# Graph attention on one core: the columns of the q and k weights reordered, and one transfer per block where there were four

## The reference, cut to what matters

```python
h = maximum(layernorm(x), 0)
q, k, v = split_heads(h @ Wq + bq), split_heads(h @ Wk + bk), split_heads(h @ Wv + bv)
scores = einsum('bhqd,bhkd->bhqk', q, k) / sqrt(32) + beta * adj
scores = where(adj > 0, scores, -9e15)
out = x + merge_heads(softmax(scores) @ v)
```

## Time and profile before

| what | value |
|---|---|
| median of 3 runs | 1079.25 us (1078.97 to 1079.58) |
| the profiled execution's own time | 1079.27 us |
| its span, first to last instruction | 1077.4 us |
| granted PE clock, mean | 0.992 of full |
| PE busy | 1020.8 us, 95% |
| DVE busy | 967.6 us, 90% |
| ACT busy | 884.5 us, 82% |
| POOL busy | 567.5 us, 53% |
| transfers of q and k into the stacks | 768 in the whole run |

### The profile page before, as it was taken

One profiled execution on the slowest core, in us unless ns is written; L12 is line 12 of the kernel. 1 busy time (PEld: TensorE's weight loads), 2 busy tenths in 40 slices (PEclk: granted clock), 3 DMA queues, 4 the chain that ended last, 5 costly groups with the idle time before them and its releaser, 6 DMA issues. The chain is left out here.

```text
span 1077.4 us, 33776 instructions
## 1 busy us (share of the span) xinstructions
PE 1020.8 (95%) x10959; PEld 709.7 (66%) x10959; DVE 967.6 (90%) x4343; ACT 884.5 (82%) x2343; POOL 567.5 (53%) x756
## 2 busy tenths in 40 slices
PE   3899999999999999999999999999999999999986
PEld 2466676666666666666666667666666666667664
DVE  6579998999899999999999999999999999999897
ACT  3378888888888888888888888888888888888887
POOL 3645655445665445565444565544565544565431
PEclk9899999999999999999999999999999999999997
DMA  5454445554444554444554444554444554444441
GB/s 156 108 132 129 113 127 139 158 134 127 107 133 132 157 138 129 111 129 136 150 140 132 111 130 129 150 145 134 130 107 132 144 150 134 130 104 135 117 116 41
DMA packets 91038, 138.79 MB, mean 129 GB/s; under 512 B 15600, under 2 KB 66288, under 8 KB 90864
## 3 DMA queue, kind: packets, MB, share of 16 engines
q1 hardware_dynamic: 90336, 135.85, 47.1%
q10 hardware_dynamic: 528, 0.79, 0.2%
HBM read 35.91 MB, written 25.17 MB: 57 GB/s over the span
## 5 line engine op out<-in xcount | busy, mean ns | idle before, releaser
L523 ACT ACTIVATE probs<-biased,neg_max 128x128 f32<-128x128 f32 x1536 | 490.5, 390 | 146.9 <-DVE neg_max L638 115.5
L437 PE MATMUL ps_p<-hT,w 128*128 128x512 f16 x1728 | 423.5, 382 | 23.9 <-DVE hT L609 18.7
L638 DVE CUSTOM_DVE_ANT_0 biased<-ps_s,mask 128x128 f32<-128x128 f32 x1536 | 353.5, 286 | 75.8 <-PE ps_s L458 74.5
L336 POOL TENSOR_TENSOR on<-on,xb 128x384 f32<-128x384 f32 x128 | 128.0, 1000 | 380.9 <-DVE on L659 380.1
L437 PEld LDWEIGHTS ps_p<-hT,w 128*128 128x128 f16 x1728 | 167.5, 98 | 175.7 <-DVE hT L609 26.1
L644 DVE TENSOR_TENSOR pT<-ps_t,pT 128x512 f16<-128x512 f32 x384 | 263.3, 686 | 0.9 <-ACT pT L548 0.9
L466 PE MATMUL ps_t<-ident,probs 128*128 128x128 f32 x1536 | 245.4, 283 | 0.1
L548 ACT ACTIVATE pT<-ps_t 128x512 f16<-128x512 f32 x384 | 220.5, 574 | 1.0 <-PE ps_t L466 1.0
L437 PE MATMUL ps_p<-w,hT 128*128 128x384 f16 x1152 | 207.6, 326 | 0.0
L458 PEld LDWEIGHTS ps_s<-k_st,q_st 96*128 96x128 f16 x1536 | 117.5, 97 | 81.3 <-DVE neg_max L638 6.9
L481 PE MATMUL ps_o<-v,pT 128*128 128x33 f16 x1536 | 157.1, 179 | 8.9 <-DVE pT L644 5.2
(11 more groups left out here) (62 smaller groups left out, 1016.8 us busy)
## 6 DMA issues: line engine op xcount, KB each, us to landing
q_st<-qT SPq DMA_DIRECT2D x384, 96.0 KB, 2.2
k_st<-kT SPq DMA_DIRECT2D x384, 96.0 KB, 2.2
out<-on SPq DMA_DIRECT2D x128, 192.0 KB, 2.1
xs<-in_x SPq DMA_DIRECT2D x31, 768.0 KB, 5.0
adjs<-in_adj SPq DMA_DIRECT2D x32, 256.0 KB, 5.0
xs<-in_x ACTq DMA_DIRECT2D x1, 768.0 KB, 7.1
k_st<-in_L_gnn_Wq SPq DMA_DIRECT2D x1, 576.0 KB, 5.6
k_st<-in_L_gnn_Wk SPq DMA_DIRECT2D x1, 576.0 KB, 9.3
```

The lines of the kernel that those rows point to most:

```text
L336: pool.tensor_tensor(on[:, j % 2, :], on[:, j % 2, :], xb[:, par, j, :], ALU.add).then_inc(added, 1)
L437: mm = pe.matmul(dst, stationary, moving, start=m == 0, stop=m == MMS - 1)
L523: act.activation(probs[:, odd, i, :], biased[:, odd, i, :], ACT.Exp, bias=neg_max[:, odd, i:i + 1], scale=-1.0).then_inc(exp_done, 1)
L638: dve.tensor_tensor_reduce(out=biased[:, odd, i, :], in0=ps_s[:, i * N:(i + 1) * N], in1=mask[:, gp, v // CH, :], scale=-1.0, scalar=3.0e3 ...
```

## The change

Columns of the q and k weights (and of their bias rows) are written in another order: old column 96i + e becomes new column 4e + i, for i from 0 to 3 and e from 0 to 95. So in column group c, partition 4d + i holds dimension d of head 3i + c. The four heads of a stack's block are then interleaved over all 128 partitions of `qT`, in the order in which 32 partitions by 4 heads are stored in `q_st`, and one transfer moves them. A step has 3 transfers for q and 3 for k. The chunk c of a graph now holds heads c, 3 + c, 6 + c, 9 + c in place of 4c to 4c + 3. The split of the weights is done in three pieces, one per row group, on ACT and on DVE, for v's too; for q's and k's the raw weights are read with a step of 96 elements between neighbours.

```diff
+        def heads_first(row):
+            return row.rearrange("p (i e) -> p e i", i=HPC)
+        def dims_first(row):
+            return row.rearrange("p (e i) -> p e i", i=HPC)
...
                 for b, part in enumerate(BLOCKS[kind]):
-                    for i in range(HPC):
-                        sp.dma_start(dst[HD * b:HD * (b + 1), par, i],
-                                     src[HD * i:HD * (i + 1), part]).then_inc(landed, 16)
+                    sp.dma_start(dst[HD * b:HD * (b + 1), par], src[:, part]).then_inc(landed, 16)
...
-                    pe.wait_ge(w_low, ("q", "k", "v").index(kind) + 1)
+                    pe.wait_ge(w_low, CH * (("q", "k", "v").index(kind) + 1))
...
-                    pe.wait_ge(q_in, 16 * 3 * HPC * (g + 1))
-                    pe.wait_ge(k_in, 16 * 3 * HPC * (g + 1))
+                    pe.wait_ge(q_in, 16 * 3 * (g + 1))
+                    pe.wait_ge(k_in, 16 * 3 * (g + 1))
...
-                    h = c * HPC + i
+                    h = i * CH + c
...
-                    wait(act, q_in if kind == "q" else k_in, 16 * 3 * HPC * s)
+                    wait(act, q_in if kind == "q" else k_in, 16 * 3 * s)
...
-                act.activation(w[:, 0, :, W_COLS[n]], w_raw[:, :, W_COLS[n]], ACT.Copy, scale=SHRINK).then_inc(w_high, 1)
+                for c in range(CH):
+                    out, raw = w[:, 0, c, W_COLS[n]], w_raw[:, c, W_COLS[n]]
+                    if n < 2:
+                        out, raw = dims_first(out), heads_first(raw)
+                    act.activation(out, raw, ACT.Copy, scale=SHRINK).then_inc(w_high, 1)
...
-            dve.scalar_tensor_tensor(out=b_scaled[:, 0, :], in0=b_row[:, 0, :], scalar=SCALE,
-                                     in1=gap[:, 0, :].bitcast(F32), op0=ALU.mult, op1=ALU.mult).then_inc(b_scaled_done, 1)
+            dve.scalar_tensor_tensor(out=dims_first(b_scaled[:, 0, :]), in0=heads_first(b_row[:, 0, :]), scalar=SCALE,
+                                     in1=heads_first(gap[:, 0, :].bitcast(F32)), op0=ALU.mult,
+                                     op1=ALU.mult).then_inc(b_scaled_done, 1)
             dve.wait_ge(qk_scaling, 9)
-            dve.tensor_tensor(b_scaled[:, 1, :], b_row[:, 1, :], gap[:, 1, :].bitcast(F32),
-                              ALU.mult).then_inc(b_scaled_done, 1)
+            dve.tensor_tensor(dims_first(b_scaled[:, 1, :]), heads_first(b_row[:, 1, :]),
+                              heads_first(gap[:, 1, :].bitcast(F32)), ALU.mult).then_inc(b_scaled_done, 1)
             def weights_low(n):
-                dve.wait_ge(w_high, n + 1)
-                dve.scalar_tensor_tensor(out=w[:, 1, :, W_COLS[n]], in0=w_raw[:, :, W_COLS[n]], scalar=SHRINK,
-                                         in1=w[:, 0, :, W_COLS[n]], op0=ALU.mult, op1=ALU.subtract).then_inc(w_low, 1)
+                for c in range(CH):
+                    low, raw, high = w[:, 1, c, W_COLS[n]], w_raw[:, c, W_COLS[n]], w[:, 0, c, W_COLS[n]]
+                    if n < 2:
+                        low, raw, high = dims_first(low), heads_first(raw), dims_first(high)
+                    dve.wait_ge(w_high, CH * n + c + 1)
+                    dve.scalar_tensor_tensor(out=low, in0=raw, scalar=SHRINK, in1=high, op0=ALU.mult,
+                                             op1=ALU.subtract).then_inc(w_low, 1)
```

## The result

| kernel | median of 4 runs, us (lowest to highest) | ratio to before (95% interval) |
|---|---|---|
| before | 1079.41 (1078.97 to 1079.77) | 1 |
| after | 1091.02 (1090.62 to 1092.04) | 1.0109 (1.0092 to 1.0127) |

The forecast was 1078.2, the range 1076.5 to 1081.6. The changed kernel lies 9.4 us above the range.

What follows compares the result with a forecast made beforehand. PE (95% busy) and DVE (90%) were taken as the bound, engines waiting in turns at set-up and last step, SP's queue a side track. Sum: 1079.27 + 0.1 - 0.7 - 0.5 = 1078.17, forecast 1078.2 us, range 1076.5 to 1081.6.

Steps and rivals of the forecast that it cites:

- With about 2 us of start and landing a spread is done 6.5 us after its first issue: Middle steps: 1.18 MB at 262 GB/s takes at least 4.5 us; 6.5 replaces 10.5, slack where nobody waits, 0 us gained.
- a rival at 0.03: PE's wait at slot 3 of each step: the large transfer is slow, each us above 12.5 costs 31; chance 0.03.
- 51.44 us: Where DVE had waited 2.7 us for x; the stall shrinks, but PE is fed from earlier work, so nothing counted.
- The last step, -0.5: Last step's k spread: PE's wait goes once the spread is done by 1043.9; gain 0.5 us, bounds 0 and -1.2.
- DVE's 0.46: Last step: DVE's wait of 0.46 us before the new scores, taken as what the end can move up.
- PE's wait of 1.19: Last step: PE waits 1.19 us for the late k spread; the bound of -1.2 if all comes back.
- Set-up, upstream +0.1: Set-up on DVE ahead of the v chain: q's low parts in three pieces take 1.4 us instead of 1.34, +0.1.
- v's parts, -0.7: Set-up: DVE may begin v's low parts after ACT's first piece; gain 0.3 to 1.3 us, 0.7 taken.
- k's 0: Set-up, k's low parts: DVE's pieces and POOL's line 381 may alternate, same work; 0 us, bounds -0.9 to +0.3.
- Reads far apart: Set-up rival: reading q's and k's raw weights 384 bytes apart costs 0.41 us a piece, giving 1080.8 us; chance 0.27.
- 0.12 to slower: Whole kernel: chance of over 1081.4 us, from a third of the far-reads rival and the slow transfer.

Runs made afterwards that it cites:

- the pieces alone: Kernel before, with only the weights' split done in three pieces on ACT and DVE, old column order, twelve transfers a spread: 1079.15 us, ratio 0.9996.
- L301: Probe on the kernel before, transfers added behind its end: 384 KB from 128 rows into partitions 0 to 31, alone; 5.2 us each.

## Why the prediction was wrong, step by step

- **"With about 2 us of start and landing a spread is done 6.5 us after its first issue"**: this is the step that failed. It took its 262 GB/s from a stretch with mixed traffic and let the shape go as a rival at 0.03. Alone, the changed kernel's spread takes 11.8 us, which is 100 GB/s with start and landing; in the kernel 11.4 to 12.9, and 15.7 for the first k spread, which stands behind other traffic. Of the 12.8 us between forecast and result this step explains about 11: the second step's 8.05, the 1.1 of the steps after it, and a last step that lost 1.4 where 0.5 were to be gained.
- **The rival with the right mechanism, at the wrong place.** I put the slow transfer's price at 31 us for every us beyond 12.5, and its decision point at 12.5 was right: the spread mostly stays just inside, and the thirty steps lose 1.1 us together. But I had priced only the middle steps. The first step, whose queue also holds two loads and whose slots have no attention, and the last, whose slots are short, decide earlier. The working had looked at 51.44 us and counted nothing, as PE was then still fed; 6 us later, where the slack was 0.14 us and not 2, it wasn't.
- **The last step, -0.5**: lost 1.4. With spreads that are fast it gains 1.2 in one trace and 0.8 in the other, so the value was too low as well: more than DVE's 0.46 comes back, and up to the whole of PE's wait of 1.19.
- **Set-up, upstream +0.1**: the pieces alone cost 1.48 against 1.34, +0.14, right. **v's parts, -0.7**: with k's 0 the sum was -0.6; the run with the pieces alone had -0.93 at the mask of step 0. The mechanism was right and the size a third low.
- **Reads far apart**: this rival, chance 0.27, was true in its mechanism. I had a price of 0.41 us a piece; it is 0.26 on DVE (0.34 for line 733 alone), and together 1.8 us (0.89 + 0.93). So the set-up is +0.89 and not -0.6. The rule on 16-byte lines of the Trainium skill (page "SBUF — State Buffer", section "Door 1: The DMA port swizzle"), which I had set against my sum, agrees with the rows: the forecast should have followed it. By itself this would have left the time inside the range.
- **The chances** gave 0.12 to slower. The trace of before had the warning: a slack of only 2 us, and a DMA share of 0.85 for 223 GB/s.

## What to carry to other kernels

Here merging transfers saved issue time on the queue, and only that. It can pay where the issue is the limit; it cost where the merged shape sent the data to few neighbouring partitions. When source and destination have different numbers of rows, time the shape alone before counting on it, from issue to landing and not by the rate of its packets; a destination spread over all partitions (every fourth here) was twice as fast as 32 neighbours. And look for the slack of a transfer in the shortest step, at the start or the end, not in the middle.

## What the hardware showed that I had not expected

- 384 KB from the same 128 rows into 32 partitions take 5.2 or 2.7 us by which 32 they are. The packets hide a part of that: those of 128 KB into 32 neighbours showed 347 GB/s while busy, yet the transfer took 2.8 us to land, and nine queued take 10.2.
- Reading has the same property: 96 KB into every fourth partition land after 2.3 us from 32 neighbouring rows and after 1.9 from every fourth. Into 32 neighbouring partitions the packets gain likewise (216 and 121 ns), yet the transfer with the faster packets landed later, 2.4 against 2.2 us alone and 2.6 against 2.2 in the kernel. Why is open; it would fit with packets that end before their bytes are written, as with L301.
- A DVE instruction of twelve elements took 2.02 us beside a POOL instruction of 3.6 us (0.17 otherwise).
- Slow transfers delayed others: stores of 192 KB landed in 4.5 us instead of 2.1.
